# Output products of a gated attention block in scaled fp16 halves instead of fp32 halves

## The reference

```python
out = out * rms * norm_w
gate = jax.nn.sigmoid(x @ Wg.T)
return gate * out @ Wo.T
...
x = _layernorm(x + _L0_attn_ref(x, ...), axis=-1)
```

## Time and profile before

| | |
|---|---|
| median of 3 runs | 1361.48 us (1359.85 to 1362.65) |
| the profiled execution | 1359.33 us |
| its span | 1357.6 us |
| TensorE busy | 1297.4 us, 96%; mean granted clock 0.988 |
| VectorE busy | 971.1 us, 72% |
| ScalarE busy | 629.1 us, 46% |
| GpSimd busy | 293.2 us, 22% |
| the chain that ended last | TensorE 79%, VectorE 7%, ScalarE 5% |

### The profile page before, as it was taken

How to read it: one execution, slowest core, us unless ns; L and a number is a source line. 1 busy time by engine, 2 the same in 40 slices (tenths; PEclk the granted TensorE clock), 3 DMA queues, 4 the chain that set the end, 5 groups by cost and what they waited for, 6 DMA issues and landing times.

```text
span 1357.6 us, 21977 instructions
## 1 busy us (share of the span) xinstructions
PE 1297.4 (96%) x7468; PEld 834.9 (61%) x7468; DVE 971.1 (72%) x1882; ACT 629.1 (46%) x1138; POOL 293.2 (22%) x213
## 2 busy tenths in 40 slices
PE   5999999999999998999999999999996999999997
PEld 3566666666666665666666656666664555555553
DVE  6875876686667675766776677767687688888763
ACT  3453443344325332533253334334354578888854
POOL 2011110011001000101010001001134555556530
PEclk9999999999999998999999999999998999999999
DMA  5100110121020101011010010001010001110000
GB/s 184 58 17 17 38 72 32 47 79 62 31 70 24 47 32 42 24 47 48 26 55 32 31 49 32 32 19 37 1 48 16 31 32 48 47 46 31 17 16 31
DMA packets 19112, 55.91 MB, mean 41 GB/s; under 512 B 2624, under 2 KB 2624, under 8 KB 18624
## 3 DMA queue, kind: packets, MB, share of 16 engines
q1 hardware_dynamic: 19008, 54.55, 11.7%
HBM read 50.35 MB, written 4.19 MB: 40 GB/s over the span
## 4 chain that ended last, share of the span: by engine, by line
PE 79%; DVE 7%; issue 6%; ACT 5%; POOL 2%; DMA 0%; DVEq 0%; POOLq 0%; ACTq 0%; SPq 0%
PE bank L400 11%; PE bank L401 11%; PE bank L402 11%; PE bank L472 4%; PE bank L415 4%; PE bank L417 4%; PE bank L416 4%; PE bank L474 4%; PE bank L473 4%; PE bank L614 3%; PE bank L615 3%; PE bank L443 2%; PE bank L460 2%; PE bank L440 1%; PE bank L624 1%
## 5 line engine op out<-in xcount | busy, mean ns | idle before, releaser
L400 PE MATMUL bank<-x_hi,w_hi 128*128 128x512 f16 x768 | 296.0, 385 | 5.2 <-DVE w_lo L1078 2.9
L401 PE MATMUL bank<-x_lo,w_hi 128*128 128x512 f16 x768 | 294.9, 384 | 3.1 <-issue 3.1
L402 PE MATMUL bank<-x_hi,w_lo 128*128 128x512 f16 x768 | 294.7, 384 | 0.0
L1124 DVE TENSOR_TENSOR resid<-resid,bank 128x512 f32<-128x512 f32 x256 | 173.1, 686 | 163.6 <-PE bank L474 162.8
L1579 POOL TENSOR_TENSOR sq_sum<-sq_sum,o_sq 128x512 f32<-128x512 f32 x64 | 101.9, 1592 | 822.5 <-ACT o_sq L758 822.5
L758 ACT ACTIVATE o_sq<-bank 128x512 f32<-128x512 f32 x64 | 38.3, 598 | 297.0 <-DVE gated L1130 297.0
L415 PE MATMUL bank<-wv_hi,x_hi 128*128 128x256 f16 x512 | 139.6, 273 | 1.0 <-DVE x_lo L1139 0.6
L416 PE MATMUL bank<-wv_lo,x_hi 128*128 128x256 f16 x512 | 139.6, 273 | 0.0
L417 PE MATMUL bank<-wv_hi,x_lo 128*128 128x256 f16 x512 | 139.6, 273 | 0.0
L400 PEld LDWEIGHTS bank<-x_hi,w_hi 128*128 128x128 f16 x768 | 76.7, 100 | 92.5 <-issue 22.1
L402 PEld LDWEIGHTS bank<-x_hi,w_lo 128*128 128x128 f16 x768 | 75.9, 99 | 92.6 <-issue 4.1
(11 more groups left out here) (174 smaller groups left out, 2668.4 us busy)
## 6 DMA issues: line engine op xcount, KB each, us to landing
w_raw<-w_ffn SPq DMA_DIRECT2D x32, 512.0 KB, 3.3
raw_a<-w_heads SPq DMA_DIRECT2D x32, 256.0 KB, 3.6
raw<-w_heads SPq DMA_DIRECT2D x15, 512.0 KB, 3.6
raw<-w_heads SPq DMA_DIRECT2D x18, 256.0 KB, 4.2
x_in<-x_rows SPq DMA_DIRECT2D x8, 512.0 KB, 4.1
out<-y_out SPq DMA_DIRECT2D x8, 512.0 KB, 2.6
resid<-x_t SPq DMA_DIRECT2D x3, 1024.0 KB, 7.9
val<-ctx_t SPq DMA_DIRECT2D x6, 512.0 KB, 3.3
```

Of the source, the lines that this page charges most:

```text
L400: mm(bk[:, :], a, c, start=kt == 0, stop=False)
L401: mm(bk[:, :], a, d, start=False, stop=False)
L402: last = mm(bk[:, :], b, c, start=False, stop=kt == KT - 1)
L1124: tt(resid[:, 4 * g + t, :], resid[:, 4 * g + t, :], YB[t % 2][:, :], ALU.add).then_inc(y_added, 1)
```

## The change

It does five things.

1. `wo_hi` and `wo_lo` become fp16. At t = 1 VectorE scales both heads' weights and takes the largest magnitude per partition (`bound_wo`); at t = 2 TensorE sums them (`wo_bound`), VectorE makes the scale (`scale_wo`) and the halves.
2. `u_hi` and `u_lo` become fp16. ScalarE sums the magnitudes of the gated unit (`sum_u`), TensorE sums over the partitions at the top of the next unit (`u_bound`, ahead of the scores), VectorE makes the scale (`scale_u`), ScalarE the high half (`split_u`, first in its next unit) and VectorE the low half, behind the masks.
3. The residual addition becomes `scalar_tensor_tensor`, which multiplies with `y_scale`.
4. The column sums of the ternary weights move behind the last unit's scores.
5. In the first row of the network the last unit's outputs move to the second tile's products, with their additions.

```diff
-        wo_hi = sb("wo_hi", [P, 2, HID], F32R, att)
+        wo_hi = sb("wo_hi", [P, 2, HID], F16, att)
...
-        u_hi = sb("u_hi", [P, GT], F32R, att)
-        u_lo = sb("u_lo", [P, GT], F32R, att)
+        u_hi = sb("u_hi", [P, GT], F16, att)
+        u_lo = sb("u_lo", [P, GT], F16, att)
+        u_abs = sb("u_abs", [P, GT], F16, att)
...
+            def u_bound(u):
+                pe.wait_ge(u_sum_ok, u + 1)
+                wait(pe, y_added, 4 * u - 1)
+                mm(UB, ones[:, :], u_sum[:, :], start=True, stop=True).then_inc(u_bound_ok, 1)
+            def wo_bound(p):
+                pe.wait_ge(wo_max_ok, p + 1)
+                wait(pe, y_added, 4 * PER_PAIR * p)
+                mm(OB, ones[:, :], wo_max[:, :], start=True, stop=True).then_inc(wo_bound_ok, 1)
...
+                if lag2:
+                    u_bound(u - 2)
+                if t == 2:
+                    wo_bound(p)
                 if lag1:
...
-                if last_pair and t == 7:
-                    column_sums()
...
-                    if first and f >= 2:
-                        output(U - 1, PAIRS - 1, 1, 2 * f - 4)
-                        output(U - 1, PAIRS - 1, 1, 2 * f - 3)
                 if first:
+                    u_bound(U - 1)
...
                 for f in range(4):
                     fc(b, 1, f)
+                    if first and f < 2:
+                        output(U - 1, PAIRS - 1, 1, 2 * f)
+                        output(U - 1, PAIRS - 1, 1, 2 * f + 1)
...
             scores(UNITS - 1, 1)
+            column_sums()
...
+            def sum_u(u):
+                act.wait_ge(gate_done, u + 1)
+                wait(act, u_bound_ok, u)
+                fn(u_abs[:, :], gated[:, :], ACT.Abs, accum_out=u_sum[:, 0:1]).then_inc(u_sum_ok, 1)
+            def split_u(u):
+                act.wait_ge(u_scale_ok, u + 1)
+                wait(act, y_done, 4 * u)
+                fn(u_hi[:, :], gated[:, :], ACT.Copy, scale=u_scale[:, 0:1]).then_inc(u_hi_ok, 1)
...
+            def bound_wo(p):
+                for i in range(2):
+                    h = 2 * p + i
+                    dve.wait_ge(woraw_in[i], 16 * p + 16)
+                    ts(raw_a[:, i, :], raw_a[:, i, :], normw[:, bass.ds(h, 1)], 0.5, ALU.mult, ALU.mult).then_inc(wo_scaled, 1)
+                dve.wait_ge(wo_scaled, 2 * p + 2)
+                wait(dve, wo_bound_ok, p)
+                v.tensor_reduce(wo_max[:, :], raw_a[:, :, :], axis=AX_X, op=ALU.max,
+                                apply_absolute_value=True).then_inc(wo_max_ok, 1)
...
+            def scale_u(u, i):
+                dve.wait_ge(u_bound_ok, u + 1)
+                ts(u_inv[:, :], UB, 1.0 / SPLIT_TOP, TINY, ALU.mult, ALU.add).then_inc(u_inv_ok, 1)
+                dve.wait_ge(u_inv_ok, u + 1)
+                v.reciprocal(u_scale[:, :], u_inv[:, :]).then_inc(u_scale_ok, 1)
+                ts(y_scale[:, :], u_inv[:, :], wo_inv[:, i:i + 1], None, ALU.mult).then_inc(y_scale_ok, 1)
+            def split_u(u):
+                dve.wait_ge(u_hi_ok, u + 1)
+                wait(dve, y_done, 4 * u)
+                stt(u_lo[:, :], gated[:, :], u_scale[:, 0:1], u_hi[:, :], ALU.mult, ALU.subtract).then_inc(u_ok, 1)
...
-                tt(resid[:, 4 * g + t, :], resid[:, 4 * g + t, :], YB[t % 2][:, :], ALU.add).then_inc(y_added, 1)
+                    dve.wait_ge(y_scale_ok, u + 1)
+                stt(resid[:, 4 * g + t, :], YB[t % 2][:, :], y_scale[:, 0:1], resid[:, 4 * g + t, :], ALU.mult,
+                    ALU.add).then_inc(y_added, 1)
...
                 stt(gated[:, :], g_t[:, :], 1.0, OT[:, :], ALU.add, ALU.mult).then_inc(gate_done, 1)
-                wait(dve, y_done, 4 * u)
-                dve.wait_ge(gate_done, u + 1)
-                v.tensor_copy(u_hi[:, :], gated[:, :]).then_inc(u_hi_ok, 1)
-                dve.wait_ge(u_hi_ok, u + 1)
-                tt(u_lo[:, :], gated[:, :], u_hi[:, :].bitcast(F32), ALU.subtract).then_inc(u_ok, 1)
...
+                if t == 2:
+                    scale_wo(p)
+                if lag2:
+                    scale_u(u - 2, i)
+                if t == 2:
+                    split_wo(p, 0)
                 if lag1:
                     if t in (1, 2):
                         dve.wait_ge(decays_ok, 2 * p + t)
                     mask(u - 1, 1 - i, 0)
                     mask(u - 1, 1 - i, 1)
+                if lag2:
+                    split_u(u - 2)
+                if lag1:
                     split_v(u - 1, (t - 1) % PER_PAIR)
```

More of the change, by code:

```diff
@@ L95, in decoder_layer @@
         dqv = sb("dqv", [P, GROUPS])
+        wo_max = sb("wo_max", [P, 2])
+        wo_inv = sb("wo_inv", [P, 2])
+        wo_scale = sb("wo_scale", [P, 2])
+        u_sum = sb("u_sum", [P, 1])
+        u_inv = sb("u_inv", [P, 1])
+        u_scale = sb("u_scale", [P, 1])
+        y_scale = sb("y_scale", [P, 1])
         stats = sb("stats", [P, 4, BT, 6])
@@ L253, in decoder_layer @@
         WB = SC[1][:, 408:408 + PROJ + 1]
+        UB = YB[0][:, 0:1]
+        OB = YB[1][:, 0:2]
         TR = bank[0:2]
@@ L509, in unit @@
                 lag2 = not first_pair or t >= 2
+                if first_pair and t == 2:
+                    pe.wait_ge(v_evac, 4)
+                if lag2:
+                    u_bound(u - 2)
+                if t == 2:
+                    wo_bound(p)
                 if lag1:
@@ L538, in unit @@
                     turn_back(0, 2, SC)
-                if first_pair and t == 2:
-                    pe.wait_ge(v_evac, 4)
                 if lag2:
@@ L694, in _ @@
             pair(PAIRS - 1, last_pair=True)
+            u_bound(UNITS - 2)
             pe.wait_ge(xqh_ok, BT)
@@ L817, in unit @@
                 lag1 = not first_unit
+                if not first_pair or t >= 2:
+                    split_u(u - 2)
                 evacuate(u, t, Q, first_unit)
@@ L941, in row @@
                         square(UNITS - 1)
+                        sum_u(UNITS - 1)
+                if first:
+                    split_u(UNITS - 1)
                 mean(b, 0)
@@ L947, in row @@
                     split_h(b, 0, f)
-                    if f == 0:
+                    if f == (2 if first else 0):
                         variance(b, 0)
@@ L977, in _ @@
             pair(PAIRS - 1, last_pair=True)
+            split_u(UNITS - 2)
             split_probs(UNITS - 1)
@@ L1081, in split_wo, with scale_wo @@
+            def scale_wo(p):
+                dve.wait_ge(wo_bound_ok, p + 1)
+                ts(wo_inv[:, :], OB, 1.0 / SPLIT_TOP, TINY, ALU.mult, ALU.add).then_inc(wo_inv_ok, 1)
+                dve.wait_ge(wo_inv_ok, p + 1)
+                v.reciprocal(wo_scale[:, :], wo_inv[:, :]).then_inc(wo_scale_ok, 1)
             def split_wo(p, i):
                 h = 2 * p + i
-                dve.wait_ge(woraw_in[i], 16 * p + 16)
+                dve.wait_ge(wo_scale_ok, p + 1)
                 wait(dve, y_done, 4 * (PER_PAIR * p - 1 + i))
-                ts(raw_a[:, i, :], raw_a[:, i, :], normw[:, bass.ds(h, 1)], 0.5, ALU.mult, ALU.mult).then_inc(wo_scaled, 1)
@@ L1129, in gate @@
                 dve.wait_ge(evacuated, PROJ * u + G + 1)
+                wait(dve, u_hi_ok, u)
+                wait(dve, u_ok, u)
                 stt(gated[:, :], g_t[:, :], 1.0, OT[:, :], ALU.add, ALU.mult).then_inc(gate_done, 1)
-                wait(dve, y_done, 4 * u)
-                dve.wait_ge(gate_done, u + 1)
-                v.tensor_copy(u_hi[:, :], gated[:, :]).then_inc(u_hi_ok, 1)
-                dve.wait_ge(u_hi_ok, u + 1)
-                tt(u_lo[:, :], gated[:, :], u_hi[:, :].bitcast(F32), ALU.subtract).then_inc(u_ok, 1)
             def split_x(g, kt):
@@ L1204, in unit @@
                     mean_squares(1, 2)
-                if t in (1, 2):
-                    split_wo(p, t - 1)
+                if t == 1:
+                    bound_wo(p)
+                if t == 2:
+                    split_wo(p, 1)
                 if t == 1 and not last_pair:
@@ L1459, in row @@
                     mean_squares(2, GROUPS)
+                    split_u(U - 1)
+                    add_y(U - 1, GROUPS - 1, 0)
+                    add_y(U - 1, GROUPS - 1, 1)
                 split_h(b, 0, 0)
@@ L1462, in row @@
                     correct(b + 1, 0)
+                if first:
+                    add_y(U - 1, GROUPS - 1, 2)
+                    add_y(U - 1, GROUPS - 1, 3)
                 split_h(b, 0, 1)
@@ L1524, in _ @@
             gate(U - 1)
-            for t in range(4):
-                add_y(U - 1, GROUPS - 1, t)
+            scale_u(U - 1, 1)
             row(0, 0, first=True)
```

15 lines of the change are left out of this document (11 added, 4 removed).

## The result

The changed kernel takes 1394.94 us (median of 4 runs, 1394.52 to 1396.4) against 1360.95 for the kernel before: 1.0255 times, 95% interval 1.0239 to 1.0271. Forecast were 1404.0 and 1376 to 1428. Its profiled execution took 1396.4 us, 37.1 more than that of before. It is slower, by less than forecast: 34 us by the medians in place of 43, and 37 by the profiled executions. One term was missed that pays back 10 us; the others together came out within some 5.

The account below looks back on a forecast made before the run. In the head units TensorE's own stream was taken as the bound, so any wait of TensorE adds in full. Terms -14 + 17 + 15 + 25 = +43 on the profiled 1359.3 gave 1402, as a median 1404 us; range 1376 to 1428.

Parts of the forecast that it names:

- Pace: Twelve output products in each head unit take 0.2155 us each in fp16 instead of 0.234: -14 us.
- Added products: TensorE's added sums over partitions, 64 for u and 8 for the output weights, 0.23 us each: +17 us.
- First new wait: At a unit's top (last value projection streamed), TensorE waits for u's sum ahead of the scores: +15 us.
- At the ternary back edges nothing: Step of the first new wait: TensorE idles 1.92 us there anyway, so the sum is ready before; no added wait.
- Second new wait: TensorE's outputs, mainly at t=1 and t=2, wait for u_lo, made on VectorE behind the decay masks: +25 us.
- u_hi is no limit.: ScalarE has u_hi ready right behind the Exp, while VectorE still masks; no time was added for it.
- The end of the head stage: Column sums and last outputs move to later places, the same work in another order: about 0.
- The addition that becomes a multiply-add: VectorE's residual addition costs the same: 686 ns before, 679 for a like multiply.
- The clock fell: Rival: the new waits lower TensorE's clock, 1.7 us each time; 1424 to 1430 us, chance 0.15.
- Only one wait shows: Rival: one of the two new waits is hidden, giving 1379 or 1389 us; chance 0.17.
- Faster: Rival: TensorE pays only for its products, as gates end over 1.3 us before the top; 1350 to 1357, chance 0.07.
- signs of being wrong: Units at t=1 and t=2 under 16 us; idle at t=3, 5 or 6; clock falling inside loops, not at edges.

Follow-up runs that it names:

- e4_plain16: Kernel before with only the halves of u and of the output weights declared fp16, no scales, bounds or new order: 1346.31 us.
- e8_all_columns: Changed kernel with the edits of e1, e2 and e3, and the column sums back where they stood before: 1361.88 us.
- e1: Changed kernel with VectorE's low half of u moved ahead of the decay wait and masks at t=1 and t=2: 1379.82 us.
- e2: e1 and, besides, ScalarE's decay Exp of t=0 and t=1 moved behind the next unit's u_hi: 1377.57 us.
- e3: Changed kernel with both bounds on TensorE moved behind the scores instead of ahead of them: 1387.88 us.
- e10_pad_both: e6_pad_pe with, besides, 65 one-column memsets on VectorE ahead of the ternary loop: 1334.21 us.
- e9_after_edge: Changed kernel with 66 one-column matmuls on TensorE ahead of the ternary loop, putting its backward branch at a block's start: 1403.32 us.
- e6_pad_pe: e4_plain16 with 18 one-column matmuls (36 instructions) on TensorE ahead of the ternary loop: 1337.58 us.

## Why the prediction was right, point by point

- **Pace, -14.** Right in size: -14.7 in e4_plain16, 13 of it in the units. Its reason, the longer weight load, isn't shown.
- **Added products, +17.** Right within 2: a quiet unit is 0.23 longer than in e4_plain16 (15.51 against 15.28), 15 over 64 units. Where a weight bound stands between fp16 products the unit got 0.07 shorter. Behind the scores, in e8_all_columns, the bound costs 0.14 (15.42).
- **First new wait, +15.** Right in mechanism and, where it was forecast, in size; some 4 short because one step failed. The group of u_abs has 621 ns and 193 for the read, taken as 630 and 198. The unit's sum starts 1.86 behind the top of t = 2 in the magnitude loop (1.9 forecast), 0.72 in the ternary loop (0.7), 0.3 at t = 3 and at t = 5 there (0.3 and 0.2), 1.1 at the exit (1.1). The step "At the ternary back edges nothing" failed: 1.2 stand there, three times, since the idle it was to hide in is gone. Missed as well: at the top of t = 2 in pair 0 the bound takes with it the wait for `v_evac` that had stood ahead of the outputs; the sum starts 1.6 behind the top there and the scores come 1.9 later than in a quiet unit.
- **Second new wait, +25.** Right in mechanism, a little large: from the end of the last fp16 product to the first output it is some 22 at the units that the forecast names. The terms of the ternary loop (1.8 and 1.7) measured 1.8 and 1.4; those of the magnitude loop's t = 1, 2.5 and 1.9, were too large: 1.6 both. Of the 22.8 in the row of waits, 4.3 stand at t = 5 and 6 of the last pair, where none was forecast. e1 and e2 take away all but 4.7, nearly all of it there.
- **"u_hi is no limit."** Wrong in the last pair. There it stands on ScalarE behind a table load and two groups of activations of the context block (4.7 together at t = 5), so the first output came 7.27 behind the top at t = 5 where it had been 4.65. The next unit grew by 3.9: a wait of 2.0 for u_lo and 1.7 of clock, 0.90 for 1.00 before (0.92 at t = 5). The last unit, which waited anyway, took 5.4 of it back: the trade is near nothing.
- **The end of the head stage, 0.** It cost 4.1 behind the last top. In the changed kernel TensorE waits 2.8 for xq_hi ahead of the last scores, a wait that the column sums had filled, and behind it the clock fell: over the 10 us behind the last top the granted clock is 0.83 where it was 1.00 before, some 1.7 us. These two are more than the 4.1; what the new order saved there I haven't taken apart. No gain shows in e8_all_columns, where the column sums are back.
- **The addition that becomes a multiply-add, "the same".** 746 ns where the addition took 686, 15 us of VectorE's time over the program; covered, since VectorE idles 148 us ahead of it.
- **The missed term: -10.** I read the 1.92 of idle at the ternary back edge as a part of the kernel that the change leaves alone. The trace of before names no releaser for it, and I did not ask whether a longer program would move it; its page has 61 packets of code, 27 more than the program, which I had not compared. It is TensorE's code coming late, and it hangs on where the loop stands in the program. The three units are 10.1 shorter (5.1, 2.5 and 2.5), net of the new wait of 1.2 each; by themselves the edges were worth some 14. That takes in idle, lower clock, and what VectorE's lateness added to it: in e4_plain16, moving TensorE's loop alone shortens the three units by 9.1.
- **The rivals.** The clock fell in units of the new waits, at the magnitude back edge and at t = 2 behind it (0.91 both, the second in the row from 319.70), as I had allowed for, and in the last pair at t = 5 and 6 and behind the last top; in e3 it fell three times more. That it would cost 1.7 at each ternary edge of the kernel before was wrong: at the third it never fell. Only one wait shows: refuted by the two rows of waits. Faster: e4 and e8 say what it would have needed, both waits gone and no bounds; its own terms (-14, +10, -3 to -8) give 1349 to 1355 and not 1350 to 1357. Of the signs of being wrong that I gave, two did show in small: 0.3 of idle at t = 3 and 5 of the ternary loop, which my own sum held, and the fall of the clock inside the magnitude loop.

The total was right to 0.7% partly by luck, because errors of both signs met. On the forecast 43 the first wait came some 4 dearer at the ternary edges, the end 4, the wait in pair 0 and a clock loss at the magnitude back edge 2 each, pace and products were 3 cheaper, and the ternary back edges gave 14: that is 38, and 37 was measured.

## What to carry to other kernels

When a scale must be found on the chip for the data of each step, count two chains, not the arithmetic: who waits for the scale at the head of an in-order queue, and behind which foreign wait the scaled half is made. Here the arithmetic was worth -14.7 + 15 and the two orders some +43; moving the calls (three of them, and the column sums) removed 33 of those. And where "issue" idle stands at the back edge of a loop, read the packets of the code queue: in these runs they exceeded the program wherever a loop was fetched again, and 36 instructions ahead of it were worth 8.7 us, more than half of what the fp16 halves gave.

The fastest version found is e10_pad_both, 1334.21 us; it does without the scales, so it serves only where the data's range allows plain fp16 halves.

## What I had not expected of the hardware

- A loop of 1622 instructions on TensorE is free at its back edge or costs, by its place, 1.7 to 2.2 us of idle ahead of its first product, then in most cases up to 2.3 us more of idle a little later or 1.7 and more of lower clock: branch at offset 36 of a block free, at 216, 250 or 0 not, and for the loop of 1667 at 124 free and at 0 not.
- A wait's row names the releaser that came last by semaphore, and can hide a code stall: in e9_after_edge it puts 1.70 down to u_abs, which was ready 0.80 before TensorE went on.
- VectorE idles 2.7 to 5.0 without a releaser at nearly every back edge in the kernel before and in every padded version, with 33 or 65 instructions ahead of its loop too. Its cause stays open; it is the next thing to look at, since behind it the edge units of e6_pad_pe are 1.5 longer than others.
